# Running layer 0's experts ahead of the attention that weighs them

## The reference

```python
x = x + L0_gnn(layernorm(x), edges)          # graph convolution over 53125 edges
# L0_ffn: y = layernorm(x)
h = y @ W_gat                                 # 4 heads x 4 experts
agg = gat_attention(h, edges2)                # 32768 edges among 2048 nodes, softmax per head
scores = mean_over_heads(layernorm(agg + b))  # one score per row and expert
g = softmax(top2(scores))                     # gates, zero for the two experts left out
x = x + sum_e g[:, e] * (gelu(y @ W1[e] + b1[e]) @ W2[e] + b2[e])   # 4 experts
x = x + L1_gnn(layernorm(x), edges)           # graph convolution, then an attention over the same edges
...
```

## Time and profile before

| | |
|---|---|
| median of 3 runs | 6434.42 us (6431.41 to 6438.44) |
| profiled execution | 6389.92 us, its span 6388.2 us |
| granted TensorE clock, mean | 0.847 |
| instructions | 61555 |
| PE, DVE, ACT, POOL busy | 70%, 49%, 33%, 24% of the span |

### The profile page before, as it was taken

One profiled execution on the slowest core, in us unless ns is written; L12 is line 12 of the kernel. 1 busy time (PEld: TensorE's weight loads), 2 busy tenths in 40 slices (PEclk: granted clock), 3 DMA queues, 4 the chain that ended last, 5 costly groups with the idle time before them and its releaser, 6 DMA issues. The chain is left out here.

```text
span 6388.2 us, 61555 instructions
## 1 busy us (share of the span) xinstructions
PE 4458.0 (70%) x18603; PEld 2933.5 (46%) x18603; DVE 3102.6 (49%) x5957; ACT 2119.6 (33%) x4137; POOL 1517.5 (24%) x1755
## 2 busy tenths in 40 slices
PE   1320280358799835878997599996685776897898
PEld 1320160221377634766776122223575445574676
DVE  8450141269511525962113898995785016444221
ACT  5100000348511103642222588786463110202222
POOL 1577656532263461100000211110110110000000
PEclk9865595668899967989999799898897898898899
DMA  9300260535100523540000344442452326361000
GB/s 378 141 1 1 67 191 1 185 101 163 53 0 0 180 81 132 188 110 1 0 0 25 125 156 136 156 155 69 174 173 67 117 83 207 105 219 31 1 0 20
DMA packets 388767, 637.45 MB, mean 100 GB/s; under 512 B 108260, under 2 KB 196833, under 8 KB 383009
## 3 DMA queue, kind: packets, MB, share of 16 engines
q1 hardware_dynamic: 351296, 627.40, 29.5%
q0 software_dynamic: 37216, 7.08, 0.7%
HBM read 529.09 MB, written 105.20 MB: 99 GB/s over the span
## 5 line engine op out<-in xcount | busy, mean ns | idle before, releaser
L1192 PE MATMUL l2g_a_agg_acc<-all_x,l2g_a_h 128*65 128x512 f32 (+1 forms) x1400 | 645.6, 586 | 22.6 <-ACT l2g_a_agg_flat L1217 21.1
L385 POOL DMA_INDIRECT table<-first_count,first_cell x416 | 405.5, 975 | 317.3 <-issue 294.5
L385 POOL DMA_INDIRECT far<-all_nil,all_far_cell x416 | 412.8, 992 | 248.1 <-DMA far<-all_nil,all_far_cell 126.4
L1290 DVE SCALAR_TENSOR_TENSOR all_x<-all_x,l2g_a_agg_counts 128x512 f32<-128x512 f32 (+1 forms) x700 | 404.9, 626 | 116.2 <-ACT all_x L1240 115.6
L1229 ACT ACTIVATE l2g_a_agg_z<-l2g_a_agg_z 128x512 f32<-128x512 f32 (+1 forms) x700 | 344.4, 538 | 140.9 <-PE l2g_a_agg_z L1172 115.7
L853 PE MATMUL l3g_agg_acc<-l3g_agg_halves,l3g_agg_exact 128*128 128x512 f32 x1250 | 303.5, 397 | 91.6 <-DVE l3g_agg_exact L906 86.7
L1240 ACT ACTIVATE all_x<-l2g_a_agg_z 128x512 f32<-128x512 f32 (+1 forms) x700 | 353.7, 569 | 0.1
L853 PE MATMUL l0g_agg_acc<-l0g_agg_halves,l0g_agg_exact 128*128 128x512 f32 x625 | 154.7, 402 | 284.4 <-DVE l0g_agg_exact L906 280.4
L1790 DVE SCALAR_TENSOR_TENSOR all_x<-l1f_moe_py,l1f_gate,all_x 128x256 f32 x200 | 96.7, 483 | 437.2 <-PE l1f_moe_py L1747 437.2
L853 PEld LDWEIGHTS l3g_agg_acc<-l3g_agg_halves,l3g_agg_exact 128*128 128x128 f32 x1250 | 236.8, 191 | 154.0 <-DVE l3g_agg_exact L906 87.5
L1192 PEld LDWEIGHTS l2g_a_agg_acc<-all_x,l2g_a_h 128*65 128x65 f32 x1400 | 170.7, 145 | 284.4 <-issue 206.9
(11 more groups left out here) (765 smaller groups left out, 9388.9 us busy)
## 6 DMA issues: line engine op xcount, KB each, us to landing
l3g_agg_counts<-table SPq DMA_DIRECT2D x250, 320.0 KB, 3.4
l2g_a_agg_counts<-table SPq DMA_DIRECT2D x300, 256.0 KB, 4.5
table<-counting_eye_rows SPq DMA_DIRECT2D x25, 1600.0 KB, 38.2
l0g_agg_counts<-table SPq DMA_DIRECT2D x125, 320.0 KB, 3.5
l1g_agg_counts<-table SPq DMA_DIRECT2D x125, 320.0 KB, 3.4
l2g_a_agg_mask<-far SPq DMA_DIRECT2D x50, 800.0 KB, 4.4
l1g_gat_agg_counts<-table SPq DMA_DIRECT2D x150, 256.0 KB, 4.4
l2g_b_agg_counts<-table SPq DMA_DIRECT2D x150, 256.0 KB, 4.4
```

The source lines that it names most:

```text
L385: pool.indirect_dma_start(self.table, bass.IndirectOffsetOnAxis(ap=self.cell[:, b, p:p + 1], axis=0), self.count(b, p), None, bounds_check ...
L1192: pe.matmul(to, rhs(t, r * per + h), p[:, u % n_p, 0:n], start=(t == 0), stop=(t == nt - 1), skip_group_check=True).then_inc(summed, 1)
L1290: dve.scalar_tensor_tensor(out=w, in0=w, scalar=1.0, in1=counts[:, b % n_counts, 0:n], op0=ALU.min, op1=ALU.mult).then_inc(weighted, 1)
```

## The change

The four experts of layer 0 run right after `l0f_ln`, before `m2` and the attention, in a new stage `experts_apart`. Its outputs with bias, not yet weighed, go to device memory (`l0f_parts`, 25 tiles x 4 experts x 128 x 256 in float32, 13.1 MB), 640 KB (5 tiles of one expert) at a time on SP's queue. DVE adds the bias `b2`, now spread over all partitions, from SBUF to the output in PSUM; PE has no bias product left. The old stage and its `turn_gates` are gone; in their place `add_parts` reads the parts back, 512 KB (a tile of four experts) at a time through a ring of 10, and DVE adds gate times part to x, 100 instructions. The order of the weight loads changes, and `l0f_settle` (the wait for them) stands ahead of the experts.

The two lists of scatters are cut anew:

| stage | before | after |
|---|---|---|
| l0g_agg | cells2 0 to 200 | cells2 0 to 104 |
| l0g_end | cells2 200 to 214 | cells2 104 to 116 |
| l0f_ln | cells2 214 to 256 | cells2 116 to 128 |
| experts | far 48 to 248 | cells2 128 to 256, far 0 to 104 |
| m2 | far 0 to 48 | far 104 to 150 |
| l0f_gat_h | none | far 150 to 162 |
| l0f_gat_agg | none | far 162 to 258, 12 behind the tops of each span |
| l0f_add (new) | | far 258 to 280 |
| l1g_ln, l1g_w | none | far 280 to 292, 292 to 306 |
| l1g_agg | far 248 to 416 | far 306 to 416 |

```diff
--- before.py
+++ after.py
@@ -1040,7 +1040,7 @@
 def attend_heads(nc, tag, c, table, far, nt, heads, width, rhs, es_rows, ec, src_rows, ed_parts, out, eps, n_counts, lag,
-                 ring):
+                 ring, beside=None):
@@ -1135,6 +1135,9 @@
                     link(pool.tensor_copy(at[:, 2:4, ms, 4], mid[:, :, ms]))
                     link(pool.tensor_tensor(at[:, 2:4, ms, 5], low, mid[:, :, ms], ALU.subtract))
                     pool.sem_inc(tops_ready, 1)
+                    if beside is not None:
+                        scatter, start, end = beside
+                        scatter.run(pool, *[start + (end - start) * (sp + i) // len(spans) for i in range(2)])
             @block.tensor
             def _(pe):
@@ -1511,7 +1514,7 @@
 def gat(nc, tag, c, fm, w, w_cols, a_src, a_dst, heads, table, far, nt, out, eps, tail=None, bias=None,
-        es_given=None, n_counts=None, lag=None, ring=None):
+        es_given=None, n_counts=None, lag=None, ring=None, beside_h=None, beside=None):
@@ -1556,11 +1559,11 @@
                     dve.tensor_copy(tail(t), ps[:, 0:w_cols])
                 return dve.tensor_copy(h[:, t, :, 0:ch], ps[:, 0:w_cols].rearrange("p (h c) -> p h c", h=heads))
-            product_nm(nc, tag + "_h", fm, wx, w_cols + 2 * heads, store)
+            product_nm(nc, tag + "_h", fm, wx, w_cols + 2 * heads, store, beside_h)
         score_rows(nc, tag + "_rows", c, ec, heads, nt, src_rows, ed_parts, ones, es_rows)
         if heads > 1:
             attend_heads(nc, tag + "_agg", c, table, far, nt, heads, ch + 1, lambda t, i: h[:, t, i, :], es_rows, ec, src_rows,
-                         ed_parts, out, eps, n_counts, lag, ring)
+                         ed_parts, out, eps, n_counts, lag, ring, beside)
         else:
             attend(nc, tag + "_agg", c, table, far, nt, ch + 1, lambda t, i: h[:, t, i, :], es_rows, ec, ones, out, eps, bias)
@@ -1794,6 +1797,119 @@
                             ny += 1
+def experts_apart(nc, tag, fm, n_e, w1, b1, w2, b2, parts, besides):
+    half, chunk, m_all = G1 * P // 2, G1 * P, 2 * KD
+    turns = [(g, e) for g in range(T // G1) for e in range(n_e)]
+    with Scope(nc, tag) as s:
+        hid = s.sb("hid", [P, 2, m_all, chunk])
+        part = s.sb("part", [P, 2, G1, D])
+        ph = s.ps("ph", [P, 2, 2, 512])
+        py = s.ps("py", [P, 4, 512])
+        with stage(nc, tag, "hid_ps", "hid_ready", "y_ps", "y_read", "part_out0", "part_out1") as (
+                block, hid_ps, hid_ready, y_ps, y_read, part_out0, part_out1):
+            part_out = [part_out0, part_out1]
+            @block.gpsimd
+            def _(pool):
+                for scatter, start, end in besides:
+                    scatter.run(pool, start, end)
+            @block.sync
+            def _(sp):
+                for i, (g, e) in enumerate(turns):
+                    sp.wait_ge(y_read, (i + 1) * G1)
+                    sp.dma_start(parts[:, g * G1:(g + 1) * G1, e, :], part[:, i % 2]).then_inc(part_out[i % 2], 16)
+                for b in range(2):
+                    sp.wait_ge(part_out[b], 16 * len(turns) // 2)
+            @block.tensor
+            def _(pe):
+                def hidden(i):
+                    g, e = turns[i]
+                    for m in range(m_all):
+                        n = i * m_all + m
+                        if n >= 2:
+                            pe.wait_ge(hid_ready, n - 1)
+                        for j in range(2):
+                            at = g * chunk + j * half
+                            for k in range(KD):
+                                last = pe.matmul(ph[:, n % 2, j, 0:half], w1[:, e, k, m * P:(m + 1) * P], fm[:, k, at:at + half],
+                                                 start=(k == 0), stop=(k == KD - 1))
+                        last.then_inc(hid_ps, 1)
+                hidden(0)
+                for i, (g, e) in enumerate(turns):
+                    if i + 1 < len(turns):
+                        hidden(i + 1)
+                    pe.wait_ge(hid_ready, (i + 1) * m_all)
+                    for tt in range(G1):
+                        n = i * G1 + tt
+                        if n >= 4:
+                            pe.wait_ge(y_read, n - 3)
+                        for k in range(m_all):
+                            last = pe.matmul(py[:, n % 4, 0:D], hid[:, i % 2, k, tt * P:(tt + 1) * P], w2[:, e, k, :],
+                                             start=(k == 0), stop=(k == m_all - 1))
+                        last.then_inc(y_ps, 1)
+            @block.scalar
+            def _(act):
+                for i, (g, e) in enumerate(turns):
+                    if i >= 2:
+                        act.wait_ge(y_ps, (i - 1) * G1)
+                    for m in range(m_all):
+                        n = i * m_all + m
+                        act.wait_ge(hid_ps, n + 1)
+                        act.activation(hid[:, i % 2, m, :].rearrange("p (j n) -> p j n", j=2), ph[:, n % 2, :, 0:half], ACT.Gelu,
+                                       bias=b1[:, e, m:m + 1]).then_inc(hid_ready, 1)
+            @block.vector
+            def _(dve):
+                for i, (g, e) in enumerate(turns):
+                    if i >= 2:
+                        dve.wait_ge(part_out[i % 2], 16 * (i // 2))
+                    for tt in range(G1):
+                        n = i * G1 + tt
+                        dve.wait_ge(y_ps, n + 1)
+                        dve.tensor_tensor(part[:, i % 2, tt, :], py[:, n % 4, 0:D], b2[:, e, :], ALU.add).then_inc(y_read, 1)
+def add_parts(nc, tag, x, gate, parts, n_e, beside=None):
+    n_ring = 10
+    with Scope(nc, tag) as s:
+        ring = s.sb("ring", [P, n_ring, n_e, D])
+        with stage(nc, tag, *[f"part_in{k}" for k in range(n_ring)], "added") as (block, *sems):
+            part_in, added = sems[:n_ring], sems[n_ring]
+            @block.sync
+            def _(sp):
+                for t in range(T):
+                    if t >= n_ring:
+                        group = (t - n_ring) // G1
+                        sp.wait_ge(added, group * G1 * n_e + G1 * (n_e - 1) + (t - n_ring) % G1 + 1)
+                    sp.dma_start(ring[:, t % n_ring], parts[:, t]).then_inc(part_in[t % n_ring], 16)
+            @block.vector
+            def _(dve):
+                for g in range(T // G1):
+                    for e in range(n_e):
+                        for tt in range(G1):
+                            t = g * G1 + tt
+                            if e == 0:
+                                dve.wait_ge(part_in[t % n_ring], 16 * (t // n_ring + 1))
+                            else:
+                                dve.wait_ge(added, (g * n_e + e - 1) * G1 + tt + 1)
+                            dve.scalar_tensor_tensor(out=x[:, t, :], in0=ring[:, t % n_ring, e, :], scalar=gate[:, t, e:e + 1],
+                                                     in1=x[:, t, :], op0=ALU.mult, op1=ALU.add).then_inc(added, 1)
+            scatter_beside(block, beside)
 def add_relu(nc, tag, x, a):
@@ -2179,35 +2295,41 @@
 def l0_gnn(nc, c, x, h, z, bias, table, dinv, scatter):
-    aggregate(nc, "l0g_agg", c, table, h, z, scale=dinv, plus=True, beside=(scatter, 0, 200))
-    add_unit_rows(nc, "l0g_end", x, z, bias, beside=(scatter, 200, 214))
+    aggregate(nc, "l0g_agg", c, table, h, z, scale=dinv, plus=True, beside=(scatter, 0, 104))
+    add_unit_rows(nc, "l0g_end", x, z, bias, beside=(scatter, 104, 116))
 def l0_ffn(nc, c, a, x, tables, dinv, scatters):
     hd, ne = 4, 4
+    cells2, far_cells = scatters
+    parts = nc.dram_tensor("l0f_parts", (P, T, ne, D), F32, kind="Internal").ap()
     with Scope(nc, "l0f") as s:
         xt = s.sb("xt", [P, KD, NP])
         gate = s.sb("gate", [P, T, ne])
-        w1 = s.sb("w1", [P, ne, KD, 2 * D])
-        b1 = s.sb("b1", [P, ne, 2 * KD])
-        w2 = s.sb("w2", [P, ne, 2 * KD, D])
-        b2 = s.sb("b2", [ne, D])
         rows = s.sb("rows", [P, 3, hd * ne])
-        normal_input(nc, "l0f", c, x, xt, [
-            [(rows[:, 0], across(a["L0_ffn_b_gat"], hd * ne)), (rows[:, 1], across(a["L0_ffn_ln_gamma"], hd * ne)),
-             (rows[:, 2], across(a["L0_ffn_ln_beta"], hd * ne)), (b2[:], a["L0_ffn_b2"]),
-             (b1[:].rearrange("p e k -> p (e k)"), vec_cols(a["L0_ffn_b1"].rearrange("e n -> (e n)")))] +
-            [(w1[:, e], a["L0_ffn_W1"][e].rearrange("(k p) n -> p k n", p=P)) for e in range(ne)] +
-            [(w2[:, e], a["L0_ffn_W2"][e].rearrange("(k p) n -> p k n", p=P)) for e in range(ne)]],
-            beside=(scatters[0], 214, scatters[0].n))
-        mask_and_degrees(nc, "m2", tables[2], T2, G2, tables[3], c.ident, None, beside=(scatters[1], 0, 48))
+        with Scope(nc, "l0fw") as q:
+            w1 = q.sb("w1", [P, ne, KD, 2 * D])
+            b1 = q.sb("b1", [P, ne, 2 * KD])
+            w2 = q.sb("w2", [P, ne, 2 * KD, D])
+            b2 = q.sb("b2", [P, ne, D])
+            normal_input(nc, "l0f", c, x, xt, [
```

(24 more changed lines are left out.)

## The result

The changed kernel took 6366.9 us (median of four runs, 6337.2 to 6376.9), the kernel before 6434.4 in the same measurement: a ratio of 0.989, 95% interval 0.985 to 0.992. So it is faster by 1.1%, but by 67 us where 208 were forecast, and 6366.9 lies outside the range of 6185 to 6272.

A forecast was written before the change was run, and what follows sets the result against it. POOL's lists of scatters were taken to set the end of four stages, costing roughly 330 us. The terms summed to -208 us, taking the median from 6434.4 to 6226 us, range 6185 to 6272.

The forecast's parts named there:

- the first term: `l0g_agg`: cut from 200 scatters to 104, the stage takes 188.7 us instead of 332.9, -144.
- 44.5 us above the profiled execution: Whole kernel: the runs' median stood this far above the profiled 6389.9 us, and the forecast carried it over.
- `add_parts`, +50 for +72: New adding stage: forecast +50 us, from 43 to 60, with additions and reads of 41.6 us each side by side.
- 1.99 us a scatter from the mask stage: Adding stage: POOL's 22 scatters at 1.99 us each make 44 us, plus 1 and a close.
- The attention, +23: Attention stage: 12 scatters behind each span's tops delay the next tops; +23 us, between 0 and 120.
- 3.3 us a span: Attention stage: what remains of 5.6 us over a 38.4 us span after DVE's give-back; 20 us over six spans.
- the 40% that DVE was to give back: Attention stage: where DVE starves, scatters run at 1.27 us, taking back about 40% of 5.6 us a span.
- The experts: Expert stage: 365 us instead of 370.3, -5, with PE's products at 354.6 and 17 us added for the writes.
- The closes behind a last scatter: Stages ended by scatters: closing behind the last one costs about 8 us, 8.1 of it ahead of the barrier.
- the free attention (0): Rival, attention stage: scatters slip in at weightings' starts and cost 0 instead of +23; 6203 us, chance 0.18.
- the expert stage bound at 471: Rival, expert stage: every scatter takes 1.99 us, so 471 us instead of 365; 6332 us in all, chance 0.04.
- the slow clock: Rival, expert stage: TensorE runs on at 1.2 GHz instead of 2.4, doubling PE's 354.6 us; slower than before, chance 0.02.

The follow-up runs named there:

- e1: The changed kernel measured again with nothing edited: 6204.3 us, 0.970 of the kernel before.
- e4: The changed kernel with no scatters in the attention stage, its 96 put back into `l1g_agg`: 6320.1 us, one run; attention took 348.6 us.
- e7: The changed kernel's new order alone, every stage holding the scatters it held in the kernel before: 6437.1 us, 1.006 of the kernel before.

## Why the prediction was wrong, point by point

The sum, with the change of each stage against the kernel before, as forecast, in the first measurement's profile, and in e1's:

| term | forecast | first | e1 |
|---|---|---|---|
| stages ahead, from 218 us to the second sort | 0 | +38 | 0 |
| `l0g_agg` | -144 | -58 | -145 |
| `l0g_end` | -3 | -3 | -3 |
| `l0f_ln` | -44 | -44 | -47 |
| experts | -5 | -11 | -11 |
| `turn_gates` | -6 | -6 | -6 |
| mask stage | -4 | -1 | -2 |
| `l0f_gat_h` | +3 | 0 | 0 |
| attention | +23 | +23 | +22 |
| `add_parts` | +50 | +72 | +72 |
| `l1g_ln`, `l1g_w` | +7 | +3 | +1 |
| `l1g_agg` | -85 | -79 | -80 |
| all else, none over 7 | 0 | +13 | +15 |
| span | -208 | -53 | -184 |

**The step that failed** is the first term, `l0g_agg` at -144, with the assumption under it that PE and DVE end at 175.2 us there and that the stages ahead keep their lengths. In the first profile DVE reached the end at 274 us, with POOL done at 167.5, and 38 more were lost ahead, 124 us together. The three repeats, each with that stage at 187.5 to 190.0 for a forecast 188.7, show that the arithmetic of scatters was right (the last ends at 178 to 181 us for 180.6) and that the loss doesn't come with the kernel each time; what it was stays open. It was no rival in the prediction, and no row of before would have spoken for it. One number could have warned: the runs' median stood 44.5 us above the profiled execution, 0.7%, and the prediction carried that over as a constant. In the later measurements before's median stands 7 to 11 above that same profile. A gap of that size was here a sign that the timed runs were not in the condition of the profile, and a reason for a wider range.

**`add_parts`, +50 for +72**, is the term that was mis-sized in every run. The prediction had seen that a scatter waits out the two-input instruction that it meets, and used it for the attention. For the adding stage, which is made of nothing but such instructions, it took 1.99 us a scatter from the mask stage. What it missed is that this chain without gaps holds a scatter as a whole: 34.4 us for one, and 15 more behind it. With a copy in five additions the stage takes the 50.0 us that were forecast.

**The attention, +23**, was right in its size and its reason: POOL's list of scatters ahead of the tops, scatters up to 3.1 us. Without them the 26 us go (e4). The knee between 10 and 12 scatters a span was not in the prediction, though its terms had it (twelve too long by 3.3 us, at 2.3 to 2.7 each). The prediction's 3.3 us a span came out in e1, though from other parts, and so partly by luck: a scatter took 2.24 us of list and not 2.67, and the 40% that DVE was to give back is not in the sum that fits.

The Trainium skill was weighed there ("SBUF — State Buffer", section "Who interferes with whom"). By its inference, two-input instructions leave a DMA issued by GpSimd alone; the runs decide against it, with 34.45 us beside additions with two inputs.

**The rest.** The experts were 6 us better: PE ends at 347 us, its products having been put at 354.6, and the stage at 359.3, some 10 behind POOL's last scatter at 349.5; that is 8 us over 342, the list without the writes, where 17 had been added for them. e7, with 32 scatters fewer, has 353.3. The closes behind a last scatter were not the 8 us taken everywhere: 9.8 there, 11 in `l1g_agg`, 4.9 in the mask stage, 2.3 in `l0g_end`. That made `l0f_gat_h`, `l1g_ln` and `l1g_w` cheaper; `l1g_agg` was 5 us dearer, about half of it by its close. So e1's whole, 24 us short of the forecast, is not one miss: `add_parts` (22), `l1g_agg` (5), the mask stage (2) and all else (15) stand against some 20 saved in other terms. Of the rivals, the free attention (0) and the expert stage bound at 471 are out; the slow clock too, with 0.99 granted in the expert stage of e1:

```profile
996.60:1355.90 359.30, 346.86 (x1440) 274.70 (x1440) 42.49 (x100) 64.72 (x81) 224.64 (x232) 0.99 0.12 37
```

## What to carry to other kernels

Work that GpSimd issues can be hidden under another engine's stage only up to the room in GpSimd's own list: take its idle time ahead of what others wait for, divide by the pitch of a scatter beside that stage's instructions, and stay under it. Where VectorE runs a long chain of two-input additions on SBUF without a gap, as in `add_parts`, try a small one-input instruction between every few of them if GpSimd has transfers to issue beside. Before you read "remote" or "issue" as a cause, see whether the trace has its semaphore records. And measure a change again, at another time, before explaining a loss in stages that it doesn't touch.
